# Attention tokenizer on one core: the order of work within a unit changed on three engines

## What is computed

```python
x = features.reshape(b, c, h, s, w, s)                  # s = 4: a patch has n = 16 pixels
reduce_feats = x.mean((3, 5)).reshape(b, c, hw).transpose(0, 2, 1)
unf = x.transpose(0, 1, 2, 4, 3, 5).reshape(b, c, hw, n).transpose(0, 2, 3, 1)
q = _ln(reduce_feats, ln_q_w, ln_q_b) @ Wq.T
kv = _ln(unf, ln_kv_w, ln_kv_b) @ Wkv.T
attn = softmax(einsum('bhpd,bhpnd->bhpn', q * scale, k), axis=-1)
aggre = einsum('bhpn,bhpnd->bhpd', attn, v)
return reduce_feats + aggre @ proj_w.T + proj_b
```

## Time and profile before

| what | value |
|---|---|
| median of 3 runs | 905.13 us (905.05 to 905.86) |
| the profiled execution, its own time | 904.89 us |
| its span in the profile | 903.1 us |
| TensorE matmul busy | 848.0 us, 94% |
| VectorE busy | 724.0 us, 80% |
| GpSimd busy | 524.6 us, 58%, nearly all of it in the first 0.6 of the span |
| ScalarE busy | 494.8 us, 55% |
| moved by DMA | 141.6 MB, nearly all of it in the first 0.6 of the span |
| granted TensorE clock, mean | 0.99 of full speed |

### The profile page before, as it was taken

One profiled execution on the slowest core, in us unless ns is written; L12 is line 12 of the kernel. 1 busy time (PEld: TensorE's weight loads), 2 busy tenths in 40 slices (PEclk: granted clock), 3 DMA queues, 4 the chain that ended last, 5 costly groups with the idle time before them and its releaser, 6 DMA issues.

```text
span 903.1 us, 23483 instructions
## 1 busy us (share of the span) xinstructions
PE 848.0 (94%) x9144; PEld 354.7 (39%) x9144; DVE 724.0 (80%) x1187; ACT 494.8 (55%) x783; POOL 524.6 (58%) x387
## 2 busy tenths in 40 slices
PE   5799999999999999999999998796999999999996
PEld 2133334334334334334334333354444444444442
DVE  5788788888788788888888888994767878778775
ACT  3555455455455455455455456356756666666662
POOL 2699899999999999999999993200212112111110
PEclk9999999999999999999999999997999999999999
DMA  9578988988988888988978956100000000000000
GB/s 375 156 200 222 260 267 227 253 270 231 253 266 231 257 260 234 256 258 240 261 247 244 259 158 158 28 1 2 1 12 13 20 17 13 24 12 13 24 13 35
DMA packets 49056, 141.60 MB, mean 157 GB/s; under 512 B 5440, under 2 KB 5440, under 8 KB 40768
## 3 DMA queue, kind: packets, MB, share of 16 engines
q1 hardware_dynamic: 48960, 140.21, 52.1%
HBM read 68.88 MB, written 4.19 MB: 81 GB/s over the span
## 4 chain that ended last, share of the span: by engine, by line
PE 37%; POOL 24%; issue 15%; DMA 9%; DVE 7%; SPq 7%; ACT 1%; POOLq 1%; DVEq 0%
DMA sb_arena<-x 7%; SPq L539 6%; POOL sb_prodv L596 5%; PE ring L1176 5%; POOL sb_rows L502 5%; PE ring L1146 4%; PE ring L917 3%; POOL sb_wgt L589 3%; PE bank_ms L1188 3%; POOL sb_score L578 3%; POOL sb_wgt L584 3%; POOL sb_rows L504 3%; PE bank_ms L889 2%; PE qp L1131 2%; PE bank_sq L1176 2%
## 5 line engine op out<-in xcount | busy, mean ns | idle before, releaser
L917 PE MATMUL ring<-sb_arena,sb_wqkv 64*64 64x512 f32 x2048 | 255.6, 603 | 4.9 <-DVE sb_prodv L1348 3.7
L1317 DVE TENSOR_TENSOR sb_prodk<-ring,sb_qbuf 128x1024 f32<-128x1024 f32 x128 | 153.3, 1220 | 18.6 <-PE ring L917 15.4
L644 POOL TENSOR_TENSOR sb_parts_q<-sb_arena,sb_const 128x512 fp32r<-128x512 f32 x15 | 15.6, 1041 | 250.6 <-DVE sb_arena L1554 250.6
L497 POOL TENSOR_TENSOR sb_rows<-sb_arena 128x2048 f32<-128x2048 f32 x31 | 141.7, 4571 | 27.2 <-DVE sb_sum L489 15.8
L1348 DVE TENSOR_TENSOR sb_prodv<-ring,sb_wbc 128x1024 f32<-128x1024 f32 x128 | 151.0, 1202 | 1.9 <-issue 1.9
L688 ACT ACTIVATE sb_xsq<-sb_arena 128x2048 f32<-128x2048 f32 x64 | 118.4, 1896 | 1.9 <-DMA sb_arena<-x 1.9
L956 PEld LDWEIGHTS qp<-sb_prodv,sb_tok_w 64*64 64x64 f32 x3072 | 88.9, 133 | 71.1 <-POOL sb_prodv L596 33.9
L917 PEld LDWEIGHTS ring<-sb_arena,sb_wqkv 64*64 64x64 f32 x2048 | 66.1, 133 | 119.2 <-issue 94.5
L956 PE MATMUL qp<-sb_prodv,sb_tok_w 64*64 64x128 f32 x3072 | 101.9, 271 | 10.6 <-POOL sb_prodv L596 8.3
L596 POOL TENSOR_TENSOR sb_prodv<-sb_prodv 128x256 f32<-128x256 f32 x128 | 93.2, 739 | 11.0 <-DVE sb_prodv L1348 11.0
L659 ACT ACTIVATE sb_means<-sb_sum 128x256 f32<-128x256 f32 x32 | 13.3, 417 | 119.2 <-POOL sb_sum L507 115.3
(11 more groups left out here) (246 smaller groups left out, 1443.0 us busy)
## 6 DMA issues: line engine op xcount, KB each, us to landing
sb_arena<-x SPq DMA_DIRECT2D x64, 1024.0 KB, 8.7
sb_wbc<-sb_wgt SPq DMA_DIRECT2D x256, 256.0 KB, 5.3
out<-sb_arena SPq DMA_DIRECT2D x16, 256.0 KB, 2.0
sb_rest_w<-rest_w SPq DMA_DIRECT2D x1, 950.5 KB, 21.5
sb_const<-const SPq DMA_DIRECT2D x1, 264.5 KB, 3.1
sb_tok_w<-tok_w SPq DMA_DIRECT2D x1, 260.5 KB, 2.9
sb_const<-const SPq DMA_DIRECT2D x1, 256.0 KB, 21.7
```

The lines of the kernel that those rows point to most:

```text
L497: eng.tensor_tensor(rows[:, :, :, :], pix[:, :, 0:8], pix[:, :, 8:16], ALU.add).then_inc(sum8_ready, 1)
L917: mm = pe.matmul(ring[slot][C * half:C * half + C, i, :], image_block(w, i), x[C * i:C * i + C, m, half, c], start=True, stop=True)
L1317: dve.tensor_tensor(by_pixel(prodk[:, c]), by_pixel(ring[c % 2][:, :, :]), q[:, :, None, :].to_broadcast([P, 2, N_PIX, G32]), ALU.mult).th ...
```

## The change

Three queues are reordered; no instruction is added or removed. On TensorE keys and projection parts alternate from the first quarter on, the first value quarter goes ahead of the scores, and the query goes ahead of squares and means, which now stand side by side between the third and the fourth value quarter. On GpSimd the last two pixel sums of a unit are done in its own step, and the first patch sum, now of unit n + 3, goes behind them to the end of the step. On VectorE the first value product goes ahead of the scores' scaling and maximum, and the third ahead of query variance and score sum.

```diff
@@ GpSimd @@
             norm_scores(0)
+            patch_sums_first(pool, 2, 2)
             def step(n, m):
-                if nxt2:
-                    patch_sums_first(pool, n + 2, (m + 2) % NF)
-                if prev:
-                    add_pixels(n - 1, 2)
-                    add_pixels(n - 1, 3)
                 if nxt2:
                     patch_sums_rest(pool, n + 2)
...
                 add_pixels(n, 1)
                 if nxt:
                     norm_scores(n + 1)
+                add_pixels(n, 2)
+                add_pixels(n, 3)
+                if nxt3:
+                    patch_sums_first(pool, n + 3, (m + 3) % NF)
             pipeline(pool, step, UNITS)
-            add_pixels(UNITS - 1, 2)
-            add_pixels(UNITS - 1, 3)
@@ TensorE @@
                     keys(n + 1, m1, 0)
-                    keys(n + 1, m1, 1)
                 if prev:
                     project(n - 1, 0)
                 if nxt:
-                    keys(n + 1, m1, 2)
+                    keys(n + 1, m1, 1)
                 if prev:
                     project(n - 1, 1)
                 if nxt:
+                    keys(n + 1, m1, 2)
                     keys(n + 1, m1, 3)
                 if prev:
                     project(n - 1, 2)
+                values(n, m, 0)
                 if nxt:
                     scores(n + 1)
-                values(n, m, 0)
                 values(n, m, 1)
+                values(n, m, 2)
                 if nxt2:
+                    query(n + 2, m2)
                     pixel_squares(n + 2, m2)
-                    query(n + 2, m2)
+                    pixel_means(n + 2, m2)
...
-                values(n, m, 2)
                 values(n, m, 3)
-                if nxt2:
-                    pixel_means(n + 2, m2)
@@ VectorE @@
                     tokens(n - 1, (m - 1) % NF)
+                value_products(n, m, 0)
                 if nxt:
                     score_scale(n + 1)
                     score_max(n + 1)
-                value_products(n, m, 0)
                 value_products(n, m, 1)
-                if nxt:
-                    score_sum(n + 1)
-                if nxt2:
-                    query_var(n + 2)
-                if nxt:
-                    score_inverse(n + 1)
...
                 value_products(n, m, 2)
+                if nxt2:
+                    query_var(n + 2)
+                if nxt:
+                    score_sum(n + 1)
+                    score_inverse(n + 1)
                 if nxt2:
                     query_scaled(n + 2)
                 value_products(n, m, 3)
```

More of the change, by code:

```diff
@@ L603, in _ @@
             norm_scores(0)
+            patch_sums_first(pool, 2, 2)
             def step(n, m):
-                prev = not isinstance(n, int) or n >= 1
                 nxt = not isinstance(n, int) or n + 1 < UNITS
                 nxt2 = not isinstance(n, int) or n + 2 < UNITS
-                if nxt2:
-                    patch_sums_first(pool, n + 2, (m + 2) % NF)
-                if prev:
-                    add_pixels(n - 1, 2)
-                    add_pixels(n - 1, 3)
+                nxt3 = not isinstance(n, int) or n + 3 < UNITS
                 if nxt2:
```

## The result

The changed kernel takes 927.59 us (median of 4 runs, 927.55 to 927.79), the kernel before took 905.50 us on the same chip (median of 4 runs, 905.05 to 908.37). The ratio on record is 1.0234, with a 95% interval from 1.0211 to 1.0257, in which the quotient of the two medians, 1.0244, lies as well: slower by 2.3%. The forecast was 926.

A forecast was written before the change was run, and what follows sets the result against it. TensorE (97.8% busy) was taken as the bound, GpSimd close behind; after the change a 17.58 us loop. 29 units at 0.67 more (19.4), plus 0.95 and 0.8, give 21.2 on 904.89: 926 us, own range 920 to 934, whole range 914 to 936.

The forecast's parts named there:

- The query's wait: TensorE before the query's matmuls: waits 0.83 us for the means, because the first patch sum now follows the fourth pixel sum.
- loop of 17.58 us: Fourth value quarter, its product, pixel sum, patch sums, means, query, squares, means matmuls, next fourth value quarter: 17.58 us a unit.
- TensorE's own work: Sum of TensorE's pieces in a unit without waits: 16.18 us in the new order, 16.34 in the old.
- V0: First of four value quarters on TensorE, placed between the last projection part and the scores; taken at 1.00 us.
- The wait before P0: TensorE before the first projection part: waits 0.57 us for the previous unit's last value product.
- The ends: Outside the 29 steady units: start-up unchanged, 0.95 us more behind the last query and 0.8 in the last units.
- wait of 0.57 before P2: Old order, TensorE before the last projection part: waits 0.57 us for GpSimd's pixel sums; goes after the change.
- rival of a late x: x transfer lands in 14 us instead of 10.4, adding 1.2 us a unit: 961 us; chance 0.04.
- two fast rivals: The two cases in which the changed kernel gets faster, about 902 and about 885 us; chance 0.12 together.
- The means come in time: No wait at the query, only at the first projection part: unit 16.75 us, kernel 902; chance 0.08.
- Neither wait is there: TensorE runs its 16.18 us of work without the two new waits: kernel about 885 us; chance 0.04.
- drain rule: TensorE: changing the tiling mode drains the engine, 0.10 us a place; by it alone the change is a gain.

The follow-up runs named there:

- squares first: Changed kernel with the squares ahead of the query again (squares, query, means, fourth value quarter): 904.22 us, ratio 0.9983 against the kernel before.
- half-sum run: Changed kernel with GpSimd's first patch sum (L497) over only half of the pixels: 897.02 us, ratio 0.9889 against the kernel before.
- keys in a pair: Changed kernel with the first two key quarters side by side ahead of the first projection part: 928.47 us, ratio 1.0237 against the kernel before.
- longer chain: Changed kernel with one more GpSimd add between the fourth pixel sum and the first patch sum: 950.54 us, ratio 1.0479 against the kernel before.
- GpSimd's part alone: Kernel before with only GpSimd's new order of pixel sums and first patch sum: 901.64 us, ratio 0.9949 against the kernel before.
- the fastest: Changed kernel with TensorE's end of step as squares, query, fourth value quarter, means: 890.43 us, ratio 0.9816 against the kernel before.

## Why the prediction was right

*The query's wait, the step that decides, was right.* Foreseen was a loop of 17.58 us, measured are 17.64 in the unit shown and 17.62 on average. The links agree to 0.06 each. Four runs show that it is this loop: taken out of the query's way (squares first) the loss is gone; shortened by 2.2 us it gives 1.04 and no more; lengthened by 0.84 it costs 0.82 in the unit shown and 0.77 on average; with the fourth value quarter in front it doesn't close. VectorE's new order was not run alone, but VectorE stands idle for 2.00 us before the product that lies on the loop (227.31), so its order adds nothing there.

*TensorE's own work was mis-sized.* I had 16.18 us from pieces of the old order, with 0.89 for a quarter before its like and 1.00 for V0. The half-sum run gives 15.94: K2 with K3 takes 1.71 there where I had 1.80, and V1 with V2 1.76 where I had 1.78; the rest is 0.05 or less a piece. The error was hidden behind the loop. It shows only in the query's wait, which is 239.41 - 236.66 - 1.77 = 2.75 - 1.77 = 0.98 by starts where I had 0.83, and it made the expected time of the half-sum run too high.

*The wait before P0* was foreseen at 0.57 and is 2.44 - 1.77 = 0.67: the product starts 1.16 instead of 1.10 behind its quarter, the hand-over takes 0.06 instead of 0.05, and V3 with K0 is taken here at 1.77 instead of 1.80. As expected, it hides in the loop of the changed kernel, and K1 would wait as long, which the keys in a pair show.

*The ends.* I had 0.95 + 0.8 = 1.75 behind the last query and measure 2.9, and the start-up, which I held fixed, is 0.7 shorter. The excess of 1.2 in the tail was not traced. Of the 0.7, 0.64 stands already at the query of unit 1, at 30.44 in the earlier trace rows and at 29.80 in the changed kernel; the longer chain has it at 30.34 with the same order of work before it. So that part is scatter between executions, and it is luck that it offsets some of the excess.

*What bounded the kernel before.* I named TensorE. That is right by its busy share, but its wait of 0.57 before P2 came from x, as GpSimd's part alone shows. The rival of a late x was wrong: no first patch sum of the changed kernel waits for x between 60 and 560 us. The forecast had seen this, from 2.3 us to spare: the first patch sum starts later in the unit, so x has more time.

*The two fast rivals.* "The means come in time" is what the half-sum run shows in TensorE's new order, with 897.0 against the 902 foreseen for that case; with the squares first it is 904.2. In the changed kernel the means don't come in time. "Neither wait is there", the case to which the drain rule of the Trainium skill (TensorEngine Tiling (Array Packing), Key Properties) leads, doesn't come about either, though the rule itself agrees with the trace: squares to means without a change of shape take 1.74 (240.22 to 241.96), means before a value quarter 1.83. The gain in TensorE's work is real, 16.34 to 15.94 in the half-sum run where 16.18 was forecast, and was eaten by waits.

## What to carry to other kernels

In a pipeline of hand-ordered queues the time of a unit is that of the longest closed loop through queues and waits, divided by the number of units that it spans, and not the busy time of the busiest engine: walk from each moved wait through every engine until you come back to the instruction you started from, and sum the starts. An operation that is moved ahead is paid by what now stands behind it; here a query that was moved ahead of two matmul groups cost 23 us because the value quarter that starts its own inputs stood behind it. Saving two changes of tile shape (0.1 us each) is worth less than the cover that a long group gives to a wait behind it.

## What the runs showed of the hardware

GpSimd's first patch sum kept its duration while VectorE's load changed: it takes 4.57 to 4.59 us in the rows of the kernel before, the changed one and the fastest, while VectorE's busy share from 200 to 300 us is 0.84, 0.80 and 0.88. And a wait in TensorE's queue looks shorter in the trace than it is: the profile gives 0.81 before the query and 0.49 before P0 where the starts give 0.98 and 0.67, since the modelled ends of matmuls reach into the wait.
